# A routing table built from one-hot rows on the chip, and half of the shared experts' tokens computed after the routed tiles

## The reference, cut to what matters

```
logits = xt @ router_w + router_b
scores = softmax(logits) + router_bias
... (two of four groups are kept, and of their experts the best two: idx)
gate = zeros((T, 16)).at[arange(T)[:, None], idx].add(scores[idx])
y = sum over the 16 experts e of gate[:, e] * ((silu(xt @ w1 + b1) * (xt @ w2 + b2)) @ w3 + b3)
z = silu(xt @ sw1 + sb1) * (xt @ sw2 + sb2) @ sw3 + sb3        # shared experts, every token
x = x + tanh(g_ffn[1]) * (y + z)
```

## Time and profile before

| | us |
|---|---|
| median of 3 runs | 1426.78 |
| lowest and highest | 1426.39, 1428.83 |
| the profiled execution's own time | 1423.45 |
| its span | 1421.7 |
| `route`, from its first instruction to PE's last | 1111 to 1224 |
| the 48 routed tiles on PE | 1227 to 1382 |
| reading back, adding, storing | 1386 to 1422 |

### The profile page before, as it was taken

One profiled execution on the slowest core, in us unless ns is written; L12 is line 12 of the kernel. 1 busy time (PEld: TensorE's weight loads), 2 busy tenths in 40 slices (PEclk: granted clock), 3 DMA queues, 4 the chain that ended last, 5 costly groups with the idle time before them and its releaser, 6 DMA issues. The chain is left out here.

```text
span 1421.7 us, 18436 instructions
## 1 busy us (share of the span) xinstructions
PE 1266.8 (89%) x5837; PEld 640.7 (45%) x5838; DVE 803.0 (56%) x1769; ACT 426.5 (30%) x1175; POOL 318.4 (22%) x210
## 2 busy tenths in 40 slices
PE   5488999999698999999999999999999789899980
PEld 1122222222264555545555455645555444577760
DVE  6888788998592256812666046741558583222216
ACT  6202412110033243323443233422433300144440
POOL 2545666672000000000000000000000035366640
PEclk9789999999799999999999999999999999999995
DMA  6000000000260010001000010000000650455539
GB/s 221 1 1 1 30 1 1 1 1 1 106 223 0 6 25 1 1 0 30 0 0 0 0 30 0 0 1 0 1 1 1 243 231 1 135 171 168 164 131 354
DMA packets 43924, 81.20 MB, mean 57 GB/s; under 512 B 21393, under 2 KB 22097, under 8 KB 43345
## 3 DMA queue, kind: packets, MB, share of 16 engines
q1 hardware_dynamic: 34864, 55.17, 10.9%
q0 software_dynamic: 8704, 25.19, 5.4%
q10 hardware_dynamic: 288, 0.00, 0.0%
HBM read 59.36 MB, written 21.01 MB: 57 GB/s over the span
## 5 line engine op out<-in xcount | busy, mean ns | idle before, releaser
L1266 POOL DMA_INDIRECT table<-ids,slot_of x32 | 31.6, 988 | 827.9 <-DVE slot_of L1491 818.4
L1011 PE MATMUL big_ps<-wo_sb,ot 128*128 128x512 f32 x384 | 176.5, 595 | 5.0 <-DVE ot L1132 5.0
L947 ACT ACTIVATE probs<-s_ps,npeak 128x128 f32<-128x128 f32 x256 | 91.8, 363 | 269.8 <-PE p_ps L1052 233.0
L1002 PE MATMUL big_ps<-ht,wq_sb 128*128 128x512 f32 x384 | 171.4, 592 | 0.0
L581 DVE TENSOR_TENSOR prod<-ring_ps,v_c 128x1024 f32<-128x1024 f32 x128 | 151.6, 1215 | 24.4 <-PE ring_ps L441 24.1
L245 POOL TENSOR_TENSOR prod<-q_p,k_c 128x2048 f32<-128x2048 f32 (+1 forms) x32 | 117.9, 3720 | 62.1 <-ACT q_p L303 62.1
L441 PE MATMUL ring_ps<-attn,sel 32*128 32x512 f32 x512 | 99.1, 652 | 32.1 <-DVE prod L581 20.1
L400 PE MATMUL out_ps<-prod,w 64*64 64x512 f32 x1024 | 127.4, 616 | 0.0
L1002 PEld LDWEIGHTS big_ps<-ht,wq_sb 128*128 128x128 f32 x384 | 70.1, 190 | 73.9 <-issue 72.8
L1011 PEld LDWEIGHTS big_ps<-wo_sb,ot 128*128 128x128 f32 x384 | 67.9, 190 | 70.6 <-issue 66.4
L1086 DVE COPY v<-big_ps 128x384 f32<-128x384 f32 x32 | 17.8, 558 | 142.6 <-PE big_ps L994 142.6
(11 more groups left out here) (213 smaller groups left out, 1795.2 us busy)
## 6 DMA issues: line engine op xcount, KB each, us to landing
wr<-in_w_routed SPq DMA_DIRECT2D x4, 3072.0 KB, 22.6
wr<-y_rows SPq DMA_DIRECT2D x32, 256.0 KB, 6.4
X<-in_x SPq DMA_DIRECT2D x4, 1024.0 KB, 9.8
ht<-in_ctx_t SPq DMA_DIRECT2D x16, 256.0 KB, 4.4
out<-X SPq DMA_DIRECT2D x16, 256.0 KB, 8.8
wq_sb<-in_wq SPq DMA_DIRECT2D x1, 3072.0 KB, 14.7
wo_sb<-in_wo SPq DMA_DIRECT2D x1, 3072.0 KB, 21.9
xn_rows<-xg SPq DMA_DIRECT2D x12, 256.0 KB, 3.1
```

The lines of the kernel that those rows point to most:

```text
L947: nc.scalar.activation(probs[:, u % 3, g2, :], s_ps[u % 2][:, g2 * P:(g2 + 1) * P], ACT.Exp, bias=npeak[:, u % 3, g2:g2 + 1], accum_out=to ...
L1002: last = nc.tensor.matmul(ps[:, :], wq_sb[:, c, (a * HC + k) * P:(a * HC + k + 1) * P], ht[:, c, :, 1, :], start=(c == 0), stop=(c == CH - 1))
L1011: last = nc.tensor.matmul(ps[:, :], ot[:, a % 2, c, k * P:(k + 1) * P], wo_sb[:, a * HC + c, :], start=(c == 0), stop=(c == HC - 1))
```

## The change

1. The table. The indirect DMAs, the DRAM tensor, its read back and the transposition go. DVE now splits each slot into a tile number and a place in the tile (four short instructions on 128 x 32), and writes two sets of one-hot rows for each of the two choices k: `place_hot` (128 x 2048) and `tile_hot` (128 x 768, in two instructions, the second multiplying by the pair's number plus one). PE multiplies them in 32 matmuls of 128 x 48 that accumulate in one bank (`tab_ps`, now in `a_ps`), one for each choice and token tile. DVE reads the result, with two more short instructions for empty slots. The one-hot rows lie in the last quarter of `wr`. So SP now loads three quarters of `wr` as before, and the fourth after `tabled`, behind the load of `b_sb`, and PE still waits for all of it at the end of `route`.
2. The shared experts. `route` does only the first 1024 tokens, in four steps with the two experts of the same 512 tokens one after the other; both `down` products of a token tile now accumulate in one bank, so that there are 8 additions into X where there were 16 for these tokens. `down` of step 0 is no longer ahead of the counting. The other 1024 tokens are done in `routed`, on PE behind the last routed tile: four `up` pairs and two `back_down`, with 4 SiLU on ACT and 4 `hidden` and 8 additions on DVE among the 32 additions of the routed results. The last eight stores of the output also wait for the shared addition.
3. `xt` is laid out by halves of the tokens, so that the biases cover only the half that `route` has used up.

```diff
 (route, SP)
+            for part in range(3):
+                wr_part(part)
             wait_rows_out(sp, range(len(xn)))
-            sp.wait_ge(scattered, 16 * 2 * T)
-            sp.dma_start(tab_sb[:], table.rearrange("(i p) o -> i (p o)", p=P)).then_inc(tab_in, 16)
             sp.wait_ge(up_done, 2 * STEPS)
             sp.dma_start(b_sb, b_in).then_inc(b_here, 16)
+            sp.wait_ge(tabled, 1)
+            wr_part(3)
 (route, POOL)
-            for k in range(2):
-                pool.wait_ge(slots_ready, k + 1)
-                for n in range(T):
-                    nc.gpsimd.indirect_dma_start(
-                        table, bass.IndirectOffsetOnAxis(ap=slot_of[:, k, n:n + 1], axis=0), ids[:, k, n:n + 1], None)\
-                        .then_inc(scattered, 16)
 (route, PE)
+            for k in (1, 2):
+                up(k, 0)
+                up(k, 1)
+            pe.wait_ge(picks_ready, 1)
...
+            down(0)
+            up(3, 0)
+            up(3, 1)
+            pe.wait_ge(silu_done, 3)
+            for k in range(2):
+                pe.wait_ge(hot_ready, k + 1)
+                for n in range(T):
+                    last = nc.tensor.matmul(tab_ps, place_hot[:, k, n, :], tile_hot[:, k, n, :],
+                                            start=(k == 0 and n == 0), stop=(k == 1 and n == T - 1))
+            last.then_inc(tabled, 1)
+            down(1)
             pe.wait_ge(wr_here, 64)
 (route, DVE)
+            for k in range(2):
+                own.mark(V.tensor_tensor(place_hot[:, k], row["place"].unsqueeze(1).to_broadcast([P, T, P]),
+                                         over(place[:, k, :], P), ALU.is_equal))
+                own.done(V.tensor_tensor(tile_hot[:, k], row["place"][:, 0:MAX_TILES].unsqueeze(1).to_broadcast([P, T, MAX_TILES]),
+                                         over(tile_no[:, k, :], MAX_TILES), ALU.is_equal))
+                V.tensor_tensor(tile_hot[:, k], tile_hot[:, k], over(token_id[:, k, :], MAX_TILES), ALU.mult)\
+                 .then_inc(hot_ready, 1)
+            add(0)
             hidden(2)
+            hidden(3)
+            dve.wait_ge(tabled, 1)
...
 (routed, PE, behind the tiles)
+            shared(0)
+            shared(1)
+            shared(2)
+            pe.wait_ge(ht_ready, MAX_TILES)
+            pe.wait_ge(y_ready, MAX_TILES)
+            back_down(0)
+            shared(3)
+            back_down(1)
 (routed, DVE, behind the tiles)
+            hidden(0)
+            combine(range(0, 4))
+            hidden(1)
+            combine(range(4, 8))
+            hidden(2)
+            combine(range(8, 12))
+            add(0)
+            combine(range(12, 14))
+            hidden(3)
+            combine(range(14, 16))
+            add(1)
```

More of the change, by code:

```diff
@@ new lines, in _ @@
+            for k in (1, 2):
+                up(k, 0)
+                up(k, 1)
+            pe.wait_ge(picks_ready, 1)
+            flat = among[:].rearrange("p t e -> p (t e)")
+            nc.tensor.matmul(prefix_ps, tri[:, :], flat, start=True, stop=True).then_inc(counted, 1)
+            nc.tensor.matmul(total_ps, ones[:, :], flat, start=True, stop=True).then_inc(counted, 1)
+            pe.wait_ge(gates_ready, 1)
+            for q in range(4):
+                last = nc.tensor.transpose(y_bank("gates")[:, q * P:(q + 1) * P],
+                                           gates[:, 4 * q:4 * q + 4, :].rearrange("p j e -> p (j e)"), ident[:, :])
@@ new lines, in _ @@
+            last.then_inc(gates_turned, 1)
+            down(0)
[9 more added lines that the diff above has]
+            down(1)
@@ L1489, in _ @@
                 own.done(V.tensor_tensor(work[:], best[:], pos[:], ALU.mult))
-                own.done(V.tensor_reduce(top[:], work[:], AX_X, ALU.add))
-                V.tensor_copy(slot_of[:, k, :], top[:]).then_inc(slots_ready, 1)
-                dve.wait_ge(slots_ready, k + 1)
-            hidden(2)
+                own.done(V.tensor_reduce(slots[:, k, :], work[:], AX_X, ALU.add))
+            own.done(V.tensor_scalar(tile_no[:], slots[:], 1.0 / P, -(P - 1) / (2.0 * P), ALU.mult, ALU.add))
@@ new lines, in _ @@
+            own.done(V.tensor_scalar_add(tile_no[:], tile_no[:], WHOLE))
+            own.done(V.tensor_scalar_add(tile_no[:], tile_no[:], -WHOLE))
+            own.done(V.scalar_tensor_tensor(place[:], tile_no[:], -float(P), slots[:], ALU.mult, ALU.add))
+            for k in range(2):
[5 more added lines that the diff above has]
+                 .then_inc(hot_ready, 1)
@@ new lines, in _ @@
+            V.tensor_scalar(tok_of[:], above, 1.0, float(T * P - 1), ALU.subtract, ALU.min).then_inc(tok_ready, 1)
+            dve.wait_ge(h_ready, 4)
+            own.done(V.tensor_tensor(te_work, ends[0:1, :].unsqueeze(1).to_broadcast([1, MAX_TILES, E]),
+                                     row["place"][0:1, 0:MAX_TILES].unsqueeze(2).to_broadcast([1, MAX_TILES, E]), ALU.is_le))
+            own.done(V.tensor_reduce(te_f[:], te_work, AX_X, ALU.add))
+            own.done(V.tensor_scalar(te[:], te_f[:], float(E - 1), None, ALU.min))
@@ L1611, in _ @@
             in_steps(act, step)
+            act.wait_ge(up_done, MAX_TILES)
+            for k in range(4):
+                act.wait_ge(shared_up, 2 * k + 1)
+                if k >= 2:
+                    act.wait_ge(shared_h, k - 1)
+                nc.scalar.activation(act_sb[:, k % 2, :], a_ps[k % 2][:, :], ACT.Silu,
+                                     bias=w_sb[:, k % SHARED, B1:B1 + 1]).then_inc(shared_silu, 1)
         @block.tensor
```

250 lines of the change are left out of this document (128 added, 122 removed).

## The result

| | us |
|---|---|
| median of 4 runs, changed kernel | 1398.62 (1394.75 to 1399.88) |
| the kernel before, on the same chip | 1426.9 (1426.39 to 1428.83) |
| ratio | 0.9786, 95% interval 0.9771 to 0.9800 |
| the profiled execution of the changed kernel | 1399.88, its span 1398.1 |

A second set of four runs gave 1397.48 us, ratio 0.9788 (0.9768 to 0.9808). The medians lie 28 us apart, and the ratio stands for some 30. The forecast was 1393, 33.7 less: right in sign and inside its range.

The account below looks back on a forecast made before the run. PE's written order was taken to bound `route`'s end, PE the tiles, and DVE's additions the tail. Tiles 41.6 us earlier less a tail 7.9 longer gave 33.7, so 1426.78 - 33.7 = 1393 us; range 1387 to 1404 (8 in 10).

Parts of the forecast that it names:

- the two lanes: In `route` ahead of the table: PE's products and DVE's one-hot rows meet within 0.3 us, at 1165.9 and 1166.2.
- The last `up` pair: On PE in `route`, just ahead of the table: `up(3)` takes 6.9 us and ends at 1165.9.
- The row of the table: In PE's table matmuls: each of 64 rows costs 0.107 us, bounded by 0.04 and 0.19.
- The tiles: Routed tiles: PE stays the bound, nothing in them changes, and they last 154.6 us as before.
- The tail: Behind the tiles: PE's shared work runs 43.5 us without a gap, and the span ends 7.9 us later.
- rival (c): In PE's tail: the clock stays low, 87 us instead of 43.5, time 1436.5, slower than before; chance 0.04.
- the table: On PE in `route`: 32 matmuls take 6.9 us, with `tabled` at 1172.8.
- rival (b): In the table: the clock falls during thin rows, the table costs 6.9 us more, time 1400; chance 0.08.
- This wait covers the rest: End of `route`: the last quarter of `wr` lands at 1184.9, 12.1 us after `tabled`, behind all other work.
- the gathers' landing: End of `route`: gathers issued from 1175.1 take 5.6 us or a little more, covered by the weight load.
- The sum: Whole kernel: 41.6 us gained less 7.9 lost gives 33.7 us less, 1393 us.
- Start of the tiles: End of `route`: the first tile starts at 1185.2 instead of 1226.76, 41.6 us earlier.

Follow-up runs that it names:

- wide_rows: Changed kernel with 28 of the 32 table matmuls given 128 moving columns rather than 48; 1396.95 us, ratio 0.9767.
- late_wait: Changed kernel with PE's wait for the last quarter of `wr` moved from the end of `route` to the fifth tile; 1396.15 us, ratio 0.9761.
- after_again: The changed kernel run again with nothing changed; 1397.48 us.
- wide_late: Changed kernel with 128-column table matmuls and the wait for the last quarter of `wr` just ahead of the first routed product; 1395.67 us, ratio 0.9764.
- one half alone: Against the kernel before: new step order and half the shared tokens behind the tiles, table still by indirect DMAs; 1427.38 us, ratio 0.9981.
- the other: Against the kernel before: one-hot table, but all eight shared steps stay in `route` and no tail; 1449.51 us, ratio 1.0143.
- table_twice: Changed kernel with the 32 table matmuls done a second time; 1410.75 us, ratio 0.9885.
- one_early: `wide_late` with one of the four gathers left at the end of `route`, three moved to the start of `routed`; 1395.94 us, ratio 0.9779.
- none_early: `wide_late` with all four gathers moved from the end of `route` to the start of `routed`; 1396.59 us, ratio 0.9776.

## Why the prediction was right, step by step

**Right.** Up to the table the two lanes came as worked out. The last `up` pair was to end at 1165.9 and did at 1166.2 (1174.96 - 8.73). DVE's wide rows took 2.29 and 0.95; PE waited 0.98 for the third bank. The row of the table costs 0.112 us at the full clock for the 0.107 that I took: the nearest row by its weights, not by its columns, was the one to take. The columns hardly count, as 48 and 128 cost the same. The Trainium skill ("TensorE: Matmul & The Clock Gate", Part 3) has a rule by which 0.147 a row was the estimate; at the full clock the trace doesn't agree, with its 0.112. The tiles took 153.7 us, 1.4 less than before; 1.0 of this lies ahead of the third tile's transposition (4.4 us from the start for 5.4), where the granted clock came back to 1.00 sooner. The tail cost 7.4 for a predicted 7.9, with PE without a gap for 43.9 us (43.5 predicted); rival (c), the low clock there, did not come.

**Mis-sized: the table.** It took 8.74 us, not 6.9, and the biases behind it 2.02, not 1.07. Of the 1.8 more in the table, 0.3 are the row's price and the rest is the clock. This is rival (b), which had a chance of 0.08 and a full price of 6.9. Against it I had set that PE has no gap ahead of the table; that is so, and it doesn't protect. The clock fell only at about 1180.4, so a quarter of the price was paid. What the profile of before showed as safe were rows of 128 to 512 columns; no row of it but the old table's one transposition had as few as 48. `wide_rows` kept the clock at 1.00 with nothing changed but the columns.

**The step that failed: "This wait covers the rest".** I made the load of the last quarter the last thing to end, 12.1 us behind the table and 0.3 more. It did take 12.4, but `late_wait` shows that it ends nothing. The step put the gathers' landing at 5.6 "or a little more" from 1175.1 and compared only the first with the load. The fourth is issued 4.0 behind the first, the first three take 7.2 to 7.6 beside the load and the fourth 6.7 (`after_again`), and `route` is not left before the last has landed. From the end of the table to the first tile it is 13.46 us after, 13.47 in `late_wait`, 13.45 in `wide_rows`, 13.48 in `wide_late`, where 12.4 was predicted. That my number came out 1.1 off rests on an accident: the two ends lie about one microsecond apart. The load still matters, through the speed of the gathers beside it. The Trainium skill ("DMA: Bandwidth & Descriptors", Anatomy of one DMA) gives an estimated 9.2 us for the 3 MB, by a fit for DMAs that GpSimd issues, where SyncE issues this one; the load took 12.4 beside the gathers, and the measurement decides.

A row of POOL ends long before its data is there: 0.95 us for the fourth gather, its last packets 6.3 us behind its issue. The Trainium skill ("Perfetto Trace Analysis", DMA Instruction — SWDGE (GPSIMD)) says so of such rows: they end when the descriptors are written. The trace agrees, and the timeline of POOL alone would never show what held `route` open.

**The sum.** Start of the tiles 38.3 instead of 41.6 us earlier (2.2 from the table, 1.1 from the gathers); tiles 1.4 shorter; tail 7.4 instead of 7.9: 32.3 instead of 33.7. The rest of the distance to the measured 1398.62 is ahead of the picks. I had assumed that nothing changes there. But of the 8.7 us, 6.4 are there already at about 150 us (the same instruction of DVE starts at 145.7 before and at 152.1 after), and all of them at 540; from there to the picks every trace takes 606.7 to 607.2 us. In the first layer of the changed kernel's trace the granted clock is lower (columns as in rows 2; the first two rows are the kernel before, the last two after):

```profile
20.00:100.00 80.00, 52.96 (x340) 12.76 (x340) 68.72 (x65) 25.32 (x36) 39.76 (x19) 0.85 0.04 15
100.00:200.00 100.00, 91.02 (x680) 24.07 (x680) 80.39 (x69) 30.04 (x36) 64.53 (x22) 1.00 0.04 11
```

```profile
20.00:100.00 80.00, 53.31 (x316) 12.90 (x316) 67.28 (x64) 26.19 (x37) 37.82 (x19) 0.79 0.05 16
100.00:200.00 100.00, 91.04 (x671) 23.86 (x667) 77.68 (x66) 28.85 (x34) 60.54 (x21) 0.97 0.03 11
```

Same code, fewer rows done in the same time, a clock of 0.79 for 0.85 and 0.97 for 1.00. The place of the picks differs from one trace to the next by up to 6 us. This clock alone doesn't tell it: in the first stretch it is 0.83 both where the picks stand at 1148.70 and where they stand at 1153.66. The trace of before was a lucky one (its time 3.3 under the median of its three runs), so part of the 8.7 is chance. Whether the rest, about 2.4 us between before's picks brought to its median (1149.4) and the mean of 11 traces (1151.8), is chance too or comes with the changed program can't be told from one trace of before. For the second speaks that the kernel before stands at 1.00 from 100 to 200 us, and all the 11 at 0.97 or 0.98; against it, that later runs of the kernel before had medians of 1427.54 to 1429.25, above the 1426.78.

## What to carry to other kernels

Before a wait is made the bound of a stage, list everything that must have ended when the stage is left, asynchronous transfers among them, each with its own landing (here POOL's gathers held the stage open, and SyncE's load did not); then undo the bound by an experiment, since a sum that comes out right may rest on the wrong term. Work taken off one engine's path pays only if the order of the others moves with it: here one half alone gave 2 to 3 us, the other cost 20, and both together gave 30. And when many small matrix products are placed in a row, their cost need not follow their columns (0.112 us a row with 48 and with 128), and the clock in and behind them belongs to the price; here more columns made them cheaper.

## What the runs showed of the hardware

- PE, busy without a pause, drops from 2.4 to 1.2 GHz in rows of 48 columns with 128 weight columns each (0.112 us a row becomes 0.213), keeps the low level for the whole 64 rows that `table_twice` added, and keeps 1.00 if 56 of the 64 rows have 128 columns (0.112 each).
- The block is not left before the gathers that POOL issued in it have landed: moving two of four out started the tiles 1.8 us earlier (40.84 to 39.08), moving three 3.5. A load that SyncE issued in it does not hold it open: in `one_early` it landed 0.8 us behind the tiles' start.
- A gather of 256 KB lands 3.5 us after its issue with no load beside it (`none_early`, where PE uses it 3.6 behind its issue), and in 6.7 to 7.7 us beside a 3 MB load and three more gathers.
- The same first 1150 us of the program differ by 6 us between traces; the differences arise in the first 540 us. Two traces of different kernels have to be laid over each other at a common instruction before stages are compared.
